# Attention: 64 rows of the staged query and key image are stored with the first head, the other 64 behind the first shift

## What is computed

```python
q, k, v = (proj(Wq), proj(Wk), proj(Wv))            # 16 heads of 8
scores = jnp.einsum('bshd,bthd->bhst', q, k) * scale  # or only within the window
attn = jax.nn.softmax(scores, axis=-1)
ctx = jnp.einsum('bhst,bthd->bshd', attn, v)
```

## Time and profile before

| | before |
|---|---|
| median of 3 runs | 2489.55 us (2487.47 to 2490.19) |
| the profiled execution, its own time | 2485.17 us |
| span of its profile, first to last instruction | 2483.4 us |
| mean granted TensorE clock | 0.896 |

### The profile page before, as it was taken

The page is one execution under the profiler, slowest core; times in us unless marked ns, Lnnn a source line. Parts: engine busy times, 40 slices in busy tenths (PEclk is TensorE's granted clock), DMA queues, the critical chain, the costliest instruction groups (busy, mean ns, idle before and its releaser), DMA issues. The chain is left out here.

```text
span 2483.4 us, 43785 instructions
## 1 busy us (share of the span) xinstructions
PE 2090.2 (84%) x15400; PEld 901.6 (36%) x15400; DVE 1809.1 (73%) x4894; ACT 1613.2 (65%) x2354; POOL 520.5 (21%) x753
## 2 busy tenths in 40 slices
PE   6497488778377799999999987848999999999696
PEld 2365255556145222222222236731222222222475
DVE  7833695442585899999999925378999999996543
ACT  3043355333244489999999963434999999999343
POOL 6176221157111000000000005720000000000075
PEclk8599699789689689999999988955999999999798
DMA  2312560211570511111011021115011011010212
GB/s 67 96 48 73 87 119 5 85 48 49 91 142 13 152 21 26 20 31 29 17 31 31 2 62 46 51 39 155 16 30 31 16 30 30 16 30 2 75 48 87
DMA packets 94743, 127.14 MB, mean 51 GB/s; under 512 B 20954, under 2 KB 72640, under 8 KB 94528
## 3 DMA queue, kind: packets, MB, share of 16 engines
q1 hardware_dynamic: 82880, 102.99, 19.0%
q0 software_dynamic: 11648, 21.36, 2.9%
HBM read 79.88 MB, written 42.40 MB: 49 GB/s over the span
## 5 line engine op out<-in xcount | busy, mean ns | idle before, releaser
L1338 ACT ACTIVATE prob<-ps 128x1024 f32<-128x1024 f32 x1024 | 989.5, 1023 | 42.4 <-PE ps L1222 22.8
L1391 DVE TENSOR_REDUCE pair_mx<-ps 128x1 f32<-128x512 f32 x1520 | 959.5, 683 | 71.1 <-PE ps L1191 69.7
L1191 PE MATMUL ps<-k_stack,q_stack 48*128 48x512 bf16 x2048 | 590.4, 402 | 27.7 <-PEq L943 8.9
L1236 PE MATMUL ps<-prob,v_head 128*32 128x512 f32 x4096 | 547.2, 606 | 1.2 <-ACT prob L1338 1.0
L1222 PE MATMUL ps<-q_stack,k_stack 51*128 51x512 bf16 x2048 | 450.3, 383 | 6.4 <-ACT prob L1338 3.8
L1191 PEld LDWEIGHTS ps<-k_stack,q_stack 48*128 48x128 bf16 x2048 | 152.7, 94 | 494.6 <-DVE pair_mx L1391 346.9
L2340 DVE TENSOR_TENSOR hid<-silu,ps 128x256 f32<-128x256 f32 (+1 forms) x190 | 87.8, 463 | 248.0 <-PE ps L2193 168.8
L1222 PEld LDWEIGHTS ps<-q_stack,k_stack 51*128 51x128 bf16 x2048 | 103.1, 93 | 302.5 <-ACT prob L1338 270.2
L1743 DVE CUSTOM_DVE_ANT_0 ps<-ps,mask 128x256 f32<-128x256 f32 (+2 forms) x512 | 179.7, 418 | 40.1 <-PE ps L1547 37.7
L1312 ACT ACTIVATE qk<-ps 128x512 f32<-128x512 f32 x264 | 157.7, 597 | 57.2 <-PE ps L1191 45.9
L2193 PE MATMUL ps<-weight_raw,block 128*128 x632 | 193.4, 429 | 0.0
(11 more groups left out here) (251 smaller groups left out, 2263.6 us busy)
## 6 DMA issues: line engine op xcount, KB each, us to landing
q_stack<-image_dram SPq DMA_DIRECT2D x88, 192.0 KB, 4.5
k_stack<-k_wide_dram SPq DMA_DIRECT2D x60, 240.0 KB, 5.2
arena<-e_rows SPq DMA_DIRECT2D x32, 256.0 KB, 4.7
k_stack<-image_dram SPq DMA_DIRECT2D x32, 192.0 KB, 4.4
image_dram<-parts SPq DMA_DIRECT2D x28, 192.0 KB, 5.4
k_wide_dram<-parts SPq DMA_DIRECT2D x2, 1800.0 KB, 17.3
image_dram<-parts SPq DMA_DIRECT2D x28, 128.0 KB, 4.9
weight_raw<-in_L_ffn_Wg_dram SPq DMA_DIRECT2D x6, 528.0 KB, 4.3
```

Source lines behind the costliest of these rows:

```text
L1191: nc.tensor.matmul(max_bank(n), rows_of(c.q_stack, b, g, ROWS, slice(t * P, (t + 1) * P)), rows_of(c.k_rows, b, g, ROWS, slice(k * CHUNK, ...
L1236: ins = nc.tensor.matmul(out, c.v_head[:, e % 2, kb, :], unit, start=(kb == 0 and e % 2 == 0), stop=(kb == TILES - 1 and e % 2 == 1), skip ...
L1338: nc.scalar.activation(c.prob[:, u % P_UNITS, :], c.ps[:, 2 * (u % 2) * CHUNK:2 * (u % 2) * CHUNK + UNIT], ACT.Exp, scale=scale).then_inc( ...
L1391: ins = nc.vector.reduce_max(mx[:, w:w + 1], max_bank(n), AX.X)
```

## The change

The first stores take 64 rows (8 heads, or 4 pairs) in the same number of transfers, in both kinds of attention. In the second block SP loads the following heads or pairs without a store or a wait for one ahead of them, in full heads 1 and 2 and with a window pairs 1 and 2. The other 64 rows are stored in six transfers once, behind the shift of head or pair 0 (with a window behind the load of pair 3, which is issued between). The head or pair that is first to need the later rows (head 8, pair 4) waits for these stores. The stores of 16 rows that stood behind each shift with a window are gone.

```diff
-def first_rows(paired):
-
-    return slice(0, (max(first_heads(paired)) + 1) * HD)
-
-
-def pair_rows_of(pair):
-
-    return slice(2 * pair * HD, 2 * (pair + 1) * HD)
+def first_rows():
+
+    return slice(0, HALF)
+
+
+def later_rows():
+
+    return slice(HALF, P)
...
-            rows = first_rows(paired)
+            rows = first_rows()
...  (full_heads_stage, SP)
                 if h >= STACKS:
                     sp.wait_ge(*st_ready.after((h - STACKS + 1) * EXP_UNITS))
+                if h == HEADS // 2:
+                    sp.wait_ge(*stored.after(2 * PARTS * 16))
                 for g in range(2):
                     load_half(sp, h, g)
 
             load_first_rest(c, sp, False)
-            for n in range(2):
-                store_parts(c, sp, n, slice(HD, P), (WHOLE, WIDE_KEYS)[n], stored)
-            sp.wait_ge(*stored.after(2 * PARTS * 16))
             for h in range(1, STACKS):
                 load_stacks(h)
             for e in range(HEADS):
                 sp.wait_ge(*rows_taken.after(e + 1))
                 store_shift(sp, e, 0)
+                if e == 0:
+                    for n in range(2):
+                        store_parts(c, sp, n, later_rows(), (WHOLE, WIDE_KEYS)[n], stored)
                 if 1 <= e < HEADS - STACKS + 1:
                     load_stacks(e + STACKS - 1)
...  (window_heads_stage, SP)
-                sp.wait_ge(*stored[h % 2].after((h + 1) // 2 * 2 * PARTS * 16))
+                if h == PAIRS // 2:
+                    sp.wait_ge(*stored.after(2 * PARTS * 16))
...
             load_first_rest(c, sp, True)
             for h in range(1, 3):
-                store_pair(h)
-            load_stacks(1)
-            store_pair(3)
+                load_stacks(h)
             for e in range(PAIRS):
                 sp.wait_ge(*rows_taken.after(e + 1))
                 store_shift(sp, e, 0)
-                for h in (2, 3) if e == 0 else (e + PAIR_STACKS - 1,):
-                    if h < PAIRS:
-                        load_stacks(h)
-                    if h >= 3 and h + 1 < PAIRS:
-                        store_pair(h + 1)
+                if e + PAIR_STACKS - 1 < PAIRS:
+                    load_stacks(e + PAIR_STACKS - 1)
+                if e == 0:
+                    for n in range(2):
+                        store_parts(c, sp, n, later_rows(), WHOLE, stored)
```

More of the change, by code:

```diff
@@ L1474, in window_heads_stage @@
     normalised = c.count("attention_kept_normalised")
-    stored = [c.count(f"proj_pair_stored_{b}") for b in range(2)]
+    stored = c.count("proj_later_stored")
     inverted = c.count("full_sums_inverted")
@@ L1805, in load_stacks @@
                     load_half(sp, h, g)
-            def store_pair(h):
-                for n in range(2):
-                    store_parts(c, sp, n, pair_rows_of(h), WHOLE, stored[h % 2])
             load_first_rest(c, sp, True)
             for h in range(1, 3):
-                store_pair(h)
-            load_stacks(1)
-            store_pair(3)
+                load_stacks(h)
             for e in range(PAIRS):
@@ L1819, in _ @@
                 store_shift(sp, e, 0)
-                for h in (2, 3) if e == 0 else (e + PAIR_STACKS - 1,):
-                    if h < PAIRS:
-                        load_stacks(h)
-                    if h >= 3 and h + 1 < PAIRS:
-                        store_pair(h + 1)
+                if e + PAIR_STACKS - 1 < PAIRS:
[3 more added lines that the diff above has]
+                        store_parts(c, sp, n, later_rows(), WHOLE, stored)
     biased.passed(len(biases))
     normalised.passed(TILES if kept else 0)
-    for b in range(2):
-        stored[b].passed((PAIRS // 2 - (1 - b)) * 2 * PARTS * 16)
+    stored.passed(2 * PARTS * 16)
     for b in range(PAIR_STACKS):
```

## The result

| | before | after |
|---|---|---|
| median of 5 runs | 2490.19 us (2487.47 to 2495.77) | 2503.55 us (2499.38 to 2507.03) |
| the profiled execution, its own time | 2485.17 us | 2507.03 us |
| ratio of the times (95% interval) | | 1.0056 (1.0044 to 1.0067) |

The account below looks back on a forecast made before the run. No engine was taken to bound the whole kernel (PE 84%, DVE 73% of the span). Windowed +2.7 and full +8.2 summed to +10.9 us, added to the median of 2489.55: about 2500 us, range 2488 to 2509.

Parts of the forecast that it names:

- The price of bytes: All stores of 64 rows: they were taken to run at 200 GB/s, between 109 and 272.
- (a): Rival, 64-row stores: they run somewhat faster, at 218 GB/s, for +3.7 us in all, 2493 us; chance 0.12.
- (c): Rival, 64-row stores: they reach the 272 GB/s of 120-row stores, for -10.3 us, 2479 us; chance 0.06.
- Part 1: Windowed attention, more rows in the first stores: the third step of pair 0 comes 6.7 us later.
- Part 2: Windowed attention, no stores ahead of pair 1: it begins 3.7 us earlier in the first window, 5.0 in the second.
- Rival (e): Windowed attention: pair 1 still waits, its loads queued behind piece 2's stores; forecast time or worse, 2505 us; chance 0.03.
- Part 3: Windowed attention, later rows behind the first shift: pair 1's second product waits 4.0 and 7.4 us for shift 1.
- rival (b): Windowed attention: shift 1 is not held, so the gain of 8.7 us stays; -0.5 us in all, 2489; chance 0.10.
- the windowed sum: Both windowed attentions: gains of 3.7 and 5.0 us against waits of 4.0 and 7.4 us, together +2.7 us.
- Part 4: Full attention: each first product comes 6.1 us later, head 1's waits of 2.36 and 1.60 us go; +8.2 us.
- Rival (d): First stores: SP is held at issue, 2 us each from the third in a run; +37 us, 2527; chance 0.05.

Follow-up runs that it names:

- the two later runs: Rows 32 to 95 first in full attention alone, 2492.18 us; 32 first rows in full and windowed attention, 2465.83 us; each against the kernel before, 2490.68 us.

## Why the prediction was right

Its direction held, and so did most of its terms and of its mechanisms. Two terms were mis-sized, one in the windows and one in full attention, and the mechanism that it named for the wait for shift 1 is not the one that the traces show. By its steps:

- **The price of bytes.** 200 GB/s taken for 64 rows; 201 and 205 measured. The rivals that stood on another rate, (a) at 218 and (c) at 272, fall with it.
- **Part 1.** The third step of pair 0 was to come 6.7 us later; it came 6.5 later (21.0 instead of 14.5 us after the first store). (The sum counts 0.590 MB for loads that hold 0.491, two of 192 KB and two of 48 KB, which is half a us; nothing turns on it.)
- **Part 2.** Pair 1 was to start 3.7 and 5.0 us earlier; it started 3.9 and 4.8 earlier, without a wait. Rival (e) falls.
- **Part 3.** A wait of 4.0 and 7.4 us for shift 1 was worked out; 3.32 and 5.09 were measured, and rival (b), that shift 1 isn't held, falls. That the later stores hold it is shown by the run that halves them. But the prediction has them hold it by standing ahead of it in SP's queue, and for (b) it names POOL's half, which goes through another. That half landed as late, 6.9 and 7.4 us after its issue, and with both halves on POOL's queue shift 1 still took 5.2 and 5.6 us to land in the second window. The shift was held by the stores on their way, whichever queue it took; how long SP's half would have been held by its place alone is open. The size came near even so, since by either mechanism the shift lands about when the last store does; that is luck. The term was 0.7 and 2.3 us too large, so the second product of pair 1 stood at -0.2 and +1.1 us, where the sum had +0.3 and +2.4. In the second window PE came to the shift 1.0 us later than worked out (48.8 us after the first store), and the shift landed 1.3 us sooner (53.9): the stretch from 692 to 700, with the load and the first later stores, moved 250 GB/s, where the sum took 194 and then 200. The 0.9 us that the sum gives to receipt stands in no row.
- **What the sum left out.** In the second window some 1.6 us more were lost behind that wait: pair 2's second product came 2.7 us late, not 1.1. In the first it was 0.9 (0.7 late, not 0.2 early). The granted clock had fallen there (last section). By luck this fills the gap that the too large term left: the windowed sum was +2.7, the stages show +3.4, the run of this part alone +0.2 at the median (-1 to +3.5).
- **Part 4, the term that was mis-sized.** The key loads came 9.69 us after the first store (9.7 worked out), the query loads 12.06 (11.7), and head 1's wait is gone. But the nine stores behind them took 6.67 us to issue (840.73 to 847.40 in SP's timeline), not 4.1. The step took 0.46 us for a store of 64 rows from stores of 16 rows; it is 0.63, and the last one waited and took 1.48. With that the first product came 9.1 us late (8.9 in the second) in place of 6.1, within the bound of 10 that was given for SP being held, and full attention costs +14.6 by the stages, +13 (9 to 18) by the run of this part alone, instead of +8.2. Rival (d), 2 us a store, overshoots by far.

So the forecast was 3.6 us under the median of after, and the term of the issue accounts for more than that: 2.57 us in each full attention. Errors of both signs met in the sum: by the runs of one part alone, full attention cost some 5 us more than forecast and the windows 2.5 us less at the median. The prediction's cause for the full attentions' loss, that the first stores are late because 64 rows move at 200 GB/s, is shown by rows 32 to 95: they give back 5.2 of the 9 us. It holds for rows 0 to 63 and not for any 64 rows in a row, since rows 32 to 95 are 64 in a row too.

## What to carry to other kernels

Before regrouping transfers, ask which of them the next engine waits for, and what will be issued while the lump is on its way: a gain at one wait was given back to a small transfer that now came while the lump was on its way, which another queue did not mend and a smaller lump did, and to the first stores, which had grown beyond what the next step needed. Cut rows by where they lie as well as by their number: here 32 first rows, then 64 that straddle row 64, beat both the 8 or 16 rows and rows 0 to 63. And a measured cost per transfer holds only for its own shape: 16 rows said 0.46 us, 64 rows took 0.63.

## What the runs showed of the hardware

**The rate of a store depends on which partitions it reads.** 64 rows at 0 to 63 or 64 to 127: 201 and 205 GB/s; 32 rows at 96 to 127: 203; 64 rows at 32 to 95: 408, and 383 and 354 in the two later runs. Beside these, 16 rows made 109 before.

**The time to issue a store on SP goes by its rows, where no stores have piled up.** Three stores of 8 rows before the change, and of 32 rows with 32 first rows in full (start, us for the three):

```profile
827.71 1.00 SPq L905 DMA_DIRECT2D image_dram<-parts  x3
```

```profile
830.01 1.37 SPq L910 DMA_DIRECT2D image_dram<-parts  x3
```

That is 0.33 and 0.46 us each; 16 rows take 0.46 as well (six in 2.76 us), 64 rows 0.63, with rows 0 to 63 and with rows 32 to 95 alike. Where stores pile up the rate shows as well: six key stores of 64 rows took 6.56 us to issue in after and 4.28 with rows 32 to 95. Why 16 and 32 rows cost the same and 64 more stays open.

**A small transfer waits for large ones that another queue has on their way.** POOL's half of a shift, 12 KB, landed 2.2 to 3.5 us after its issue in the kernel before. With the later stores of SP's queue on their way it was 6.9 and 7.4 us in after, and 5.2 and 5.6 us for the two halves in the second window with both on POOL's queue.

**A wait can cost more than itself.** Behind the 5.09 us that PE waited in after's second window, the next stretches and their granted clock:

```profile
709.00:717.00 8.00, 6.54 (x98) 4.31 (x100) 3.55 (x22) 2.90 (x4) 0.98 (x4) 0.57 0.56 114
717.00:725.00 8.00, 6.79 (x137) 4.51 (x136) 6.94 (x43) 3.94 (x6) 1.07 (x3) 1.00 0.04 8
```

In the first 8 us the clock granted was 0.57 on the mean, so for most of it the lower level of 1.2 GHz; in the next 8 us it was 2.4 GHz. The products with the values that follow pair 1's first second product took 1.51 us in the first stretch (at 711.85) and 0.87 us before (at 706.57). The kernel before, which had no wait there, was granted 1.00 at the same work:

```profile
704.00:712.00 8.00, 7.31 (x162) 5.07 (x160) 7.18 (x46) 4.54 (x7) 1.43 (x6) 1.00 0.75 154
```

This is also the place where part of the 9.3 us come from by which PE's busy time grew.
